# Source scores of every second group gathered from a table in memory instead of looked up with one-hots

## The chip, the core and the metric

The kernel runs on one core of a Trainium2 chip. The metric is the device time of one execution in microseconds. The kernel before takes 1955.77 us, the median of three runs (1955.05 to 1958.15).

## What is computed

Four graph layers follow each other on 1250 nodes with 512 features and 20000 edges, each with a residual sum and a layer norm. The change lies in the second one, graph attention with 8 heads. Its core, cut from the reference:

```
h = (x @ W.T).reshape(n, 8, 64)
e_src = einsum('ehd,hd->eh', h[src], a_src)
e_dst = einsum('ehd,hd->eh', h[dst], a_dst)
e = leaky_relu(e_src + e_dst, 0.2) * (1 + et_emb[edge_type]) * edge_weight
alpha = softmax of e over the edges of a target node
out = scatter_add(dst, h[src] * alpha)
```

For each edge the scores `e_src` (8 numbers that depend on its source node alone) and `e_dst` (8 numbers that depend on its target node) are needed. Each node's scores are small products that the stage before has made.

## The kernel before

The edges are sorted by the block of 128 nodes that holds their target and padded to 176 tiles ("slots") of 128 edges, one edge on a partition. Two slots are a pair with one target block. Stages stand one after another, each a block of programs for the five engines, with a barrier of all engines between two stages.

The stage of the change is `edge_scores` (L1734). It reads the node scores `est` and `edt` (128 partitions x 10 blocks x 8 heads) and fills `es_out` and `ed_out` (128 edges x 176 slots x 8 heads). It goes by groups of four slots, 44 groups in 11 steps of four (`u` = 0 to 3). For one group:

- DVE builds (`build`, L1787, L1792) a one-hot of the source node within its block, a one-hot of the target node within its block, both 128 x 512, and a small one-hot of the source's block.
- PE turns both one-hots (`turn`, L1854, 8 transposes), ACT copies the result to SBUF (L1838).
- PE looks up (`look`, L1865, L1868): the turned source one-hot times the scores of all ten blocks (80 columns, in three bfloat16 parts), the turned target one-hot times those of the pair's block (8 columns, three parts); 24 matmuls in all.
- DVE copies the target scores (L1803), masks the ten candidates of the source with the block one-hot (`mask`, L1805) and sums them (`take`, L1813).

The engines overlap by order: PE turns group g, then looks up g - 1; DVE builds g, masks g - 2, sums g - 3. One-hots, turned one-hots and lookups have two buffers each.

In steps 1 to 8 the stage also mixes the basis of the last layer (`Basis`, L169): 16 pieces of 2 MB are loaded by SP into two buffers (L197), PE multiplies a piece in two halves (L211), one after each lookup, so that a piece takes two groups; ACT copies the results and stores them (L220, L224). SP issues a piece when both halves of the piece before it in the same buffer have been multiplied. GpSimd has no program in the stage. The stage after it, `attention_weights` (L1891), starts with GpSimd's gathers of `h` rows (L674), with an index tile that the changed stage now reads too.

Of the kernel before, what the change touches and what calls it, by code (L numbers as in the profile page):

```python
# [23 lines left out]
P = 128  # L24
N, E, D = 1250, 20000, 512
NB = -(-N // P)
NP = NB * P
# [13 lines left out]
H, DH = 8, 64  # L41
# [1680 lines left out]
GS = 4  # L1722
# [11 lines left out]
def edge_scores(nc, name, C, identb, est, edt, src_lo, src_block, loc, pair_block, es_out, ed_out,  # L1734
                basis):

# [4 lines left out]
    U = 4  # L1741
    STEPS = SLOTS // GS // U
    with ExitStack() as ctx:
# [13 lines left out]
        built, turned, copied, looked = sem("built"), sem("turned"), sem("copied"), sem("looked")  # L1757
        masked, taken = sem("masked"), sem("taken")
        basis.begin(ctx, sem)
        mixing = lambda i: 1 <= i <= Basis.STEPS if isinstance(i, int) else True  # L1760
# [11 lines left out]
        @block.sync  # L1772
        def _(sp):
            basis.load(sp)

        @block.vector
        def _(v):
# [5 lines left out]
            def build(i, u):  # L1783
                wait(v, turned, i * U + (u - 1))
                s = bass.ds((i * U + u) * GS, GS)
                for n, col in ((0, src_lo), (1, loc)):
                    nc.vector.tensor_tensor(oh[:, u % 2, n, :, :],  # L1787
                                            C.f("iota_p").unsqueeze(1).to_broadcast([P, GS, P]),
                                            col[:, s].unsqueeze(2).to_broadcast([P, GS, P]),
                                            ALU.is_equal).then_inc(built, 1)  # L1790
                wait(v, masked, i * U + (u - U + 1))
                nc.vector.tensor_tensor(ohb[:, u, :, :],  # L1792
                                        C.f("iota_p")[:, 0:NB].unsqueeze(1).to_broadcast([P, GS, NB]),
                                        src_block[:, s].unsqueeze(2).to_broadcast([P, GS, NB]),
                                        ALU.is_equal).then_inc(built, 1)

            def mask(i, u):

                g = i * U + u
                v.wait_ge(built, g * 3 + 3)  # L1800
                v.wait_ge(looked, g + 1)
                wait(v, taken, g - 1)
                nc.vector.tensor_copy(ed_out[:, bass.ds(g * GS, GS), :],  # L1803
                                      pl[:, u % 2, ES:ES + ED].rearrange("p (s h) -> p s h", h=H))
                nc.vector.tensor_tensor(  # L1805
                    mine[:, u % 2, :, :, :],
                    pl[:, u % 2, 0:ES].rearrange("p (s b h) -> p s h b", h=H, b=NB),
                    ohb[:, u, :, :].unsqueeze(2).to_broadcast([P, GS, H, NB]), ALU.mult).then_inc(masked, 1)

            def take(i, u):  # L1810
                g = i * U + u
                v.wait_ge(masked, g + 1)
                nc.vector.tensor_reduce(es_out[:, bass.ds(g * GS, GS), :], mine[:, u % 2, :, :, :],  # L1813
                                        AX.X, ALU.add).then_inc(taken, 1)
# [16 lines left out]
        @block.scalar  # L1831
        def _(act):
            def step(i):
                for u in range(U):
                    g = i * U + u
                    act.wait_ge(turned, g + 1)
                    wait(act, looked, g - 1)
                    nc.scalar.copy(ohT[:, u % 2, :, :, :], pT[:, u % 2, :, :, :]).then_inc(copied, 1)  # L1838
                    if mixing(i):
                        basis.store(act, i - 1, u // 2, u % 2)  # L1840
            steps(act, step)
            basis.end_store(act)

        @block.tensor
        def _(pe):
            pe.wait_ge(tables, 1)

            def turn(i, u):
                g = i * U + u
                pe.wait_ge(built, g * 3 + 2)  # L1850
                wait(pe, copied, g - 1)
                for n in range(2):
                    for s in range(GS):
                        ins = nc.tensor.transpose(pT[:, u % 2, n, s, :], oh[:, u % 2, n, s, :], identb[:, :])  # L1854
                ins.then_inc(turned, 1)

            def look(i, u):
# [5 lines left out]
                for s in range(GS):  # L1863
                    for n in range(3):
                        nc.tensor.matmul(pl[:, u % 2, s * NB * H:(s + 1) * NB * H], ohT[:, u % 2, 0, s, :],  # L1865
                                         flat(s3[:, n, :, :]), start=n == 0, stop=n == 2)
# [198 lines left out]
def gnn(nc, ins, consts, out):  # L2065
# [5 lines left out]
    tab = {n: dram(f"tab_{n}", s) for n, s in {  # L2071
        "q": [NP, D], "h": [NP, D],
        "w1": [REL * BCH, D * D // BCH], "w2": [REL * BCH, D * D // BCH]}.items()}
    VECS = ["L0_gnn_b", "L1_gnn_ln_gamma", "L1_gnn_ln_beta", "L2_gnn_bias", "L2_gnn_gamma", "L2_gnn_beta",
            "L3_gnn_bias1", "L3_gnn_bias2"]
    with ExitStack() as top:
# [180 lines left out]
        with ExitStack() as ctx:  # L2257
            es, ed = (ctx.enter_context(nc.sbuf_tensor(f"edge_{n}", [P, SLOTS, H], F32)) for n in ("e_src", "e_dst"))
            edge_scores(nc, "scores", C, identb, est, edt, src_lo, src_block, loc["dst"], pairs["dst"], es, ed, basis[1])
            attention_weights(nc, "att", C, es, ed, factor, loc["dst"][:, :], block_of_pair[:, :],  # L2260
# [88 lines left out]
```

## Time and profile before

| | |
|---|---|
| median of three runs | 1955.77 us |
| profiled execution | 1963.35 us |
| its span | 1961.5 us |
| PE busy | 1613.1 us (82%) |
| DVE busy | 1164.8 us (59%) |
| ACT busy | 471.8 us (24%) |
| POOL (GpSimd) busy | 684.4 us (35%) |

Busy times are sums over the span and come from stages with different limits. The stage of edge scores lies between about 973 and 1114 us. TensorE's granted clock is given as a share of its full speed of 2.4 GHz; 0.5 is the level of 1.2 GHz. PEld is TensorE's weight load, POOL is GpSimd. A name with a q (SPq, POOLq) is the engine's sequencer, which issues transfers and waits.

### The profile page before, as it was taken

What the parts mean: (1) busy time and instruction counts of PE and PEld (TensorE: products, weight loads), DVE (VectorE), ACT (ScalarE), POOL (GpSimd) and SP (SyncE); (2) the same over time, 40 slices, a digit from 0 to 9 for tenths busy, and PEclk for the clock granted to TensorE, in tenths of its full rate; (3) what the DMA queues carried; (4) which work ended last, traced back from release to release, by engine and by line L of the source; (5) the groups of instructions that cost most, each with busy time, mean ns of one, the idle gap of its engine ahead of it and who ended that gap; (6) DMA issues with size and microseconds to landing.
All of it is one profiled execution on the core that took longest, in us unless ns stands there. A gap on an engine that the chain in (4) does not pass through costs nothing. (4 is left out here: it accounts for less than half of the span.)

```text
span 1961.5 us, 27790 instructions
## 1 busy us (share of the span) xinstructions
PE 1613.1 (82%) x7565; PEld 984.4 (50%) x7566; DVE 1164.8 (59%) x2302; ACT 471.8 (24%) x884; POOL 684.4 (35%) x605
## 2 busy tenths in 40 slices
PE   6751886777588999998888639988498899999998
PEld 6641553334443555554555425544245545874486
DVE  5678656886356777776477776665773822113222
ACT  4300112433311555554344310000110111001100
POOL 0002834887265776661000247776340010000000
PEclk9999988999679999999989669999799999999999
DMA  0002885001920776673279327777104301430033
GB/s 25 0 0 86 279 294 189 1 1 54 350 85 38 206 206 187 186 176 71 96 282 353 130 76 210 208 211 188 35 1 129 108 0 38 171 134 1 1 133 134
DMA packets 76201, 248.91 MB, mean 127 GB/s; under 512 B 14758, under 2 KB 28439, under 8 KB 68203
## 3 DMA queue, kind: packets, MB, share of 16 engines
q1 hardware_dynamic: 38474, 147.06, 21.0%
q0 software_dynamic: 34592, 96.87, 18.7%
q10 hardware_dynamic: 3072, 4.20, 0.7%
q8 instruction: 33, 0.54, 0.1%
q14 instruction: 30, 0.24, 0.0%
HBM read 215.91 MB, written 32.00 MB: 126 GB/s over the span
## 5 line engine op out<-in xcount | busy, mean ns | idle before, releaser
L645 POOL DMA_INDIRECT tab_slots<-slot_words,slot_address x160 | 220.5, 1378 | 286.4 <-issue 231.0
L1424 PE MATMUL dense_pY<-weights,dense_xT_block 128*128 128x512 f32 x640 | 284.4, 601 | 0.0
L674 POOL DMA_INDIRECT e_rows<-tab_h,idx_h x176 | 174.9, 994 | 297.8 <-POOLq L50 220.1
L1472 PE MATMUL dense_pY<-parts,dense_number 128*128 128x512 f32 x1000 | 238.4, 400 | 6.9 <-DMA dense_number<-tab_edges_to 6.8
L975 POOL DMA_INDIRECT e_rows<-tab_q,idx_q x192 | 182.4, 950 | 98.5 <-issue 39.8
L1472 PEld LDWEIGHTS dense_pY<-parts,dense_number 128*128 128x128 f32 x1000 | 189.3, 190 | 54.7 <-DMA dense_number<-tab_edges_to 8.0
L768 PE MATMUL e_pS<-e_rows,e_onehot_ring 128*128 128x512 f32 x352 | 195.4, 646 | 21.0 <-DVE e_rows L744 18.5
L1424 PEld LDWEIGHTS dense_pY<-weights,dense_xT_block 128*128 128x128 f32 x640 | 121.6, 194 | 143.5 <-issue 143.2
L1048 PE MATMUL e_pS<-e_rows,e_onehot_f 128*128 128x512 f32 x384 | 181.4, 596 | 0.0
L858 PE MATMUL count_pA<-count_onehot_d,count_onehot_s 128*128 128x512 f16 (+1 forms) x576 | 119.6, 355 | 46.7 <-DVE count_onehot_d L836 44.6
L744 DVE TENSOR_TENSOR e_rows<-e_rows,e_pW 128x1024 f32<-128x1024 f32 x88 | 107.3, 1220 | 68.9 <-DMA e_rows<-tab_h,idx_h 68.9
L992 DVE TENSOR_TENSOR e_rows<-e_rows,e_pP 128x1024 f32<-128x1024 f32 x96 | 117.1, 1220 | 7.4 <-DMA e_rows<-tab_q,idx_q 6.6
L836 DVE TENSOR_SCALAR count_onehot_d<-count_iota,dst_of_src 128x1280 f16<-128x1280 f16 x192 | 109.8, 614 | 18.8 <-PE count_pA L858 17.2
L1442 DVE SCALAR_TENSOR_TENSOR parts<-dense_pY,dense_gates,parts 128x512 fp32r<-128x512 f32 x40 | 28.2, 747 | 146.8 <-ACT parts L1434 146.8
L858 PEld LDWEIGHTS count_pA<-count_onehot_d,count_onehot_s 128*128 128x128 f16 x576 | 56.3, 98 | 110.5 <-issue 97.2
L770 PEld LDWEIGHTS e_pN<-edge_weights,e_onehot_ring 128*128 128x128 f32 x352 | 67.9, 193 | 86.0 <-issue 86.0
L1231 PE MATMUL n_pY<-weights,n_xT_block 128*128 128x512 f32 x240 | 109.6, 608 | 0.0
L1017 ACT ACTIVATE e_rows<-e_rows 128x1024 f32<-128x1024 f32 x96 | 101.7, 1059 | 5.6 <-DVE e_rows L992 5.6
L1001 DVE TENSOR_TENSOR acc<-e_pS,acc 128x512 f32 x96 | 66.4, 692 | 58.2 <-PE e_pS L1048 58.2
L1048 PEld LDWEIGHTS e_pS<-e_rows,e_onehot_f 128*128 128x128 f32 x384 | 72.7, 189 | 55.8 <-issue 47.5
L1651 DVE TENSOR_TENSOR acc<-dense_pY,acc 128x512 f32<-128x512 f32 x20 | 13.8, 692 | 145.9 <-PE dense_pY L1472 145.9
L617 PE MATMUL src_pO<-src_onehot_s,src_onehot_p 125*128 125x192 f32 x320 | 68.1, 366 | 32.7 <-DVE src_onehot_s L606 32.7
(312 smaller groups left out, 2459.8 us busy)
## 6 DMA issues: line engine op xcount, KB each, us to landing
basis_piece<-in_L_gnn_basis_pieces SPq DMA_DIRECT2D x32, 2048.0 KB, 8.0
dense_number<-tab_edges_from SPq DMA_DIRECT2D x20, 1280.0 KB, 5.5
tab_edges_from<-counts_turned SPq DMA_DIRECT2D x10, 1280.0 KB
tab_edges_to<-counts_total SPq DMA_DIRECT2D x10, 640.0 KB
dense_number<-tab_edges_to SPq DMA_DIRECT2D x10, 640.0 KB, 4.6
tab_w<-basis_wout ACTq DMA_DIRECT2D x128, 32.0 KB
weights<-tab_w SPq DMA_DIRECT2D x4, 1024.0 KB, 6.6
weights<-in_L_gnn_W_T SPq DMA_DIRECT2D x3, 1024.0 KB
```

The costliest lines, as they stand in the source:

```text
L645: pool.indirect_dma_start(self.table, bass.IndirectOffsetOnAxis(self.address[:, t:t + 1], 0), self.words[:, t, :], None).then_inc(self.pla ...
L674: pool.indirect_dma_start(self.rows[:, q, s, :], None, self.table, bass.IndirectOffsetOnAxis(self.idx[:, j * 2 + s:j * 2 + s + 1], 0)).the ...
L744: nc.vector.tensor_tensor(r, r, pW[:, bass.ds(i * 16 + u * 2, 2), :].unsqueeze(3).to_broadcast([P, 2, H, DH]), ALU.mult).then_inc(weighted, 1)
L768: nc.tensor.matmul(flat(pS[:, bass.ds(bank[u], 1), :]), ohr[:, u % 4, s, :], rows[:, u, s, :], start=False, stop=True, skip_group_check=True)
L836: nc.vector.tensor_scalar(ohd[:, u % RING, :], iota[:, :], dst[:, bass.ds(t, 1)], None, ALU.is_equal).then_inc(built, 1)
L858: ins = nc.tensor.matmul(flat(pA[:, bass.ds(bank[u], 1), a:b]), ohs[:, h, u, :], ohd[:, u % RING, a:b], start=False, stop=True, skip_group ...
L975: pool.indirect_dma_start(rows[:, q, s, :], None, q_table, bass.IndirectOffsetOnAxis(idx[:, j * 2 + s:j * 2 + s + 1], 0)).then_inc(got[q], 16)
L992: nc.vector.tensor_tensor(rows[:, u, :, :], rows[:, u, :, :], pP[:, u % 2, :, :], ALU.add).then_inc(summand, 1)
L1048: ins = nc.tensor.matmul(pS[:, u % 2, :], ohf[:, u, s, :], rows[:, u, s, :], start=s == 0, stop=s == 1)
L1231: ins = nc.tensor.matmul(py[:, k, w, :], xt[:, k, c, :], weights[w][0][:, c, :], start=c == 0, stop=c == 3)
L1424: ins = self.nc.tensor.matmul(self.banks.at(g), self.xt[:, b % 2, c, :], weights[:, c, :], start=c == 0, stop=c == 3)
L1472: ins = self.nc.tensor.matmul(self.banks.at(self.first + b), self.number[:, b % 2, r * NB + k, :], self.parts[r][n][:, k, :], start=k == 0 ...
```

## The change

The groups with `u` 0 and 2 stay as they are. In the groups with `u` 1 and 3 DVE builds the target one-hot alone, PE turns and looks up only that, ACT copies half as much, and the masking and the sum are left out. For their 88 slots GpSimd gathers the source scores with an indirect DMA for each slot, 128 rows of 8 float32 numbers, from a table in memory. SP writes this table (40 KB) at the start of the stage; GpSimd waits for that, and at the end for all its gathers.

```diff
@@ edge_scores
+        est_out, es_in = sem("est_out"), sem("es_in")
+        looked_up = lambda u: u % 2 == 0
+        built_ahead = (0, 3, 4, 7)
...
         @block.sync
         def _(sp):
+            sp.dma_start(est_table.rearrange("(b p) h -> p b h", p=P), est[:, :, :]).then_inc(est_out, 16)
             basis.load(sp)
+            sp.wait_ge(est_out, 16)
+
+        @block.gpsimd
+        def _(pool):
+            pool.wait_ge(est_out, 16)
+            gathered = [g * GS + s for g in range(STEPS * U) if not looked_up(g % U) for s in range(GS)]
+            for s in gathered:
+                pool.indirect_dma_start(es_out[:, s, :], None, est_table,
+                                        bass.IndirectOffsetOnAxis(idx[:, s:s + 1], 0)).then_inc(es_in, 16)
+            pool.wait_ge(es_in, 16 * len(gathered))
...
             def build(i, u):
...
-                for n, col in ((0, src_lo), (1, loc)):
+                for n, col in ((0, src_lo), (1, loc))[0 if looked_up(u) else 1:]:
...
+                if not looked_up(u):
+                    return
...
             def mask(i, u):
...
+                if not looked_up(u):
+                    ins.then_inc(masked, 1)
+                    return
...
             def take(i, u):
+                if not looked_up(u):
+                    return
...
-                    nc.scalar.copy(ohT[:, u % 2, :, :, :], pT[:, u % 2, :, :, :]).then_inc(copied, 1)
+                    ends = slice(0 if looked_up(u) else 1, 2)
+                    nc.scalar.copy(ohT[:, u % 2, ends, :, :], pT[:, u % 2, ends, :, :]).then_inc(copied, 1)
...
-                for n in range(2):
+                for n in range(0 if looked_up(u) else 1, 2):
                     for s in range(GS):
                         ins = nc.tensor.transpose(pT[:, u % 2, n, s, :], oh[:, u % 2, n, s, :], identb[:, :])
...
-                    for n in range(3):
+                    for n in range(3 if looked_up(u) else 0):
                         nc.tensor.matmul(pl[:, u % 2, s * NB * H:(s + 1) * NB * H], ohT[:, u % 2, 0, s, :],
```

On GpSimd, between the gathers of the first convolution (`e_rows` from `tab_q`) and those of the attention weights (`e_rows` from `tab_h`), the row order now is (the lines moved by up to 22):

```order
 L975 DMA e_rows<-tab_q,idx_q 128x512 x192
 L952 UNCONDITIONAL_BRANCH
-L49 ISA x3
-L1932 UNCONDITIONAL_BRANCH
+L49 ISA x2
+L1781 UNCONDITIONAL_BRANCH
+L1786 DMA edge_e_src<-tab_est,idx_h 128x8 x88
+L1743 UNCONDITIONAL_BRANCH
+L49 ISA
+L1954 UNCONDITIONAL_BRANCH
 L674 DMA e_rows<-tab_h,idx_h 128x512 x16
```

Where GpSimd passed from one barrier to the next, 88 gathers into `edge_e_src` (`es_out`) stand between the two.

On PE, in the loop of the mixing steps, the kernel before has this from one multiply of a piece to the next (`scores_pT` are the transposes, `scores_pLook` the lookups, `basis_ps` the multiplies):

```order
L211 MATMUL basis_ps<-basis_piece,basis_mix 32x512 x4
L1850 ISA
L1854 MATMUL scores_pT<-identb,scores_onehots 128x128 x8
L1859 ISA
L1859 TENSOR_LOAD pair_block_dst
...
L1865 MATMUL scores_pLook<-scores_source,scores_onehotsT 128x80 x3
L1868 MATMUL scores_pLook<-scores_target,scores_onehotsT 128x8 x3
L211 MATMUL basis_ps<-basis_piece,basis_mix 32x512 x4
```

In the changed kernel, from the second multiply of a piece over the first of the next one to its second:

```order
L1876 MATMUL scores_pT<-identb,scores_onehots 128x128 x8
...
L1890 MATMUL scores_pLook<-scores_target,scores_onehotsT 128x8 x4
L207 REGISTER_ALU
L77 REGISTER_ALU
L211 MATMUL basis_ps<-basis_piece,basis_mix 32x512 x4
L1872 REGISTER_ALU
L1876 MATMUL scores_pT<-identb,scores_onehots 128x128 x4
...
L1887 MATMUL scores_pLook<-scores_source,scores_onehotsT 128x80 x3
L1890 MATMUL scores_pLook<-scores_target,scores_onehotsT 128x8 x3
L77 REGISTER_ALU
L211 MATMUL basis_ps<-basis_piece,basis_mix 32x512 x4
```

Between a piece's first and second multiply stand the four transposes of a gathered group and the full lookup of the group before it; between its second and the next piece's first, eight transposes and the short lookup of a gathered group.

## Rows read from the trace of the kernel before

**Rows 1.** Windows: length, busy us (instructions) by engine, clock, DMA share, GB/s.

```profile
970.00:988.60 18.60, 10.22 (x136) 8.90 (x136) 12.70 (x36) 5.11 (x6) 0.00 (x0) 0.57 0.62 241
988.60:1089.00 100.40, 86.97 (x1254) 51.30 (x1251) 71.83 (x189) 47.09 (x62) 0.00 (x0) 0.96 0.83 313
1089.00:1114.00 25.00, 18.08 (x280) 15.81 (x279) 18.61 (x50) 8.58 (x9) 0.00 (x0) 0.63 0.04 7
```

**Rows 2.** Timeline of DVE at the stage's end: start us, us, instruction, idle before.

```profile
1112.25 0.48 DVE L1805 TENSOR_TENSOR scores_of_own_block<-scores_pLook,scores_onehot_block 128x320 f32<-128x320 f32 x1
1112.65 0.87 DVE L1813 TENSOR_REDUCE edge_e_src<-scores_of_own_block 128x32 f32<-128x320 f32 x2
1114.26 0.25 DVE L1961 TENSOR_SCALAR att_mask<-loc_dst 128x176 f32<-128x176 f32 x1 [0.74 <-PEq L50]
```

**Rows 3.** Landing of the basis loads; timeline of their issues, multiplies and transposes.

```profile
DMA to landing us min/median/max: 7.7/8.0/12.5
...
1020.49 6.23 SPq L197 DMA_DIRECT2D basis_piece<-in_L_gnn_basis_pieces  x2
1021.99 1.07 PE L211 MATMUL basis_ps<-basis_piece,basis_mix 128*32 128x512 f32 x8
1022.99 0.62 PE L1854 MATMUL scores_pT<-identb,scores_onehots 128*128 128x128 bf16 x8
1025.10 1.06 PE L211 MATMUL basis_ps<-basis_piece,basis_mix 128*32 128x512 f32 x8
...
1028.58 1.06 PE L211 MATMUL basis_ps<-basis_piece,basis_mix 128*32 128x512 f32 x8 [0.15 <-DMA basis_piece<-in_L_gnn_basis_pieces]
```

**Rows 4.** Timeline of PE: first multiply of the basis, and one group in the tail.

```profile
988.60 1.94 PE L211 MATMUL basis_ps<-basis_piece,basis_mix 128*32 128x512 f32 x8
...
1099.07 1.01 PE L1854 MATMUL scores_pT<-identb,scores_onehots 128*128 128x128 bf16 x8
1100.50 0.36 PE L1865 MATMUL scores_pLook<-scores_source,scores_onehotsT 128*128 128x80 bf16 x3 [0.42 <-DVE scores_of_own_block L1805]
...
1101.77 1.01 PE L1854 MATMUL scores_pT<-identb,scores_onehots 128*128 128x128 bf16 x8
```

**Rows 5.** Lines of GpSimd's indirect DMAs in two stages; shortest scatter by its line.

```profile
L975 POOL DMA_INDIRECT e_rows<-tab_q,idx_q x192 | 182.4, 950 | 98.5 <-issue 39.8 <-PE e_pS L1048 36.4 <-SPq L952 22.3
...
L645 POOL DMA_INDIRECT tab_slots<-slot_words,slot_address x88 | 129.6, 1472 | 75.5 <-POOLq L50 49.0 <-issue 26.5
...
L645 POOL DMA_INDIRECT tab_slots<-slot_words,slot_address x160: 1172/1238/2172, 183.5 to 506.2; - x160
```

**Rows 6.** Timeline of GpSimd and DVE at the start of the next stage.

```profile
1116.14 1.74 POOL L674 DMA_INDIRECT e_rows<-tab_h,idx_h  x1 [0.30 <-issue]
1118.18 1.36 POOL L674 DMA_INDIRECT e_rows<-tab_h,idx_h  x1 [0.30 <-issue]
...
1115.43 1.63 DVE L1966 TENSOR_TENSOR edge_e_src<-edge_e_src,edge_e_dst 128x1408 f32<-128x1408 f32 x1
1117.10 1.62 DVE L1967 SCALAR_TENSOR_TENSOR edge_e_src<-edge_e_src 128x1408 f32<-128x1408 f32 x1
```

**Rows 7.** Timeline of DVE: the builds of one group in the mixing stretch.

```profile
1020.38 0.68 DVE L1787 TENSOR_TENSOR scores_onehots<-const_table,src_lo 128x512 bf16<-128x512 f32 x1
1020.98 0.68 DVE L1787 TENSOR_TENSOR scores_onehots<-const_table,loc_dst 128x512 bf16<-128x512 f32 x1
1021.59 0.19 DVE L1792 TENSOR_TENSOR scores_onehot_block<-const_table,src_block 128x40 f32<-128x40 f32 x1
```

**Rows 8.** Landing of L975; scatter queue, 183 to 300 us; issues: KB, us to landing.

```profile
DMA to landing us min/median/max: 3.3/3.7/7.8
...
q0 software_dynamic: 1792, 0.12, 3.0%
...
basis_mix<-in_L_gnn_att_mix SPq DMA_DIRECT2D x1, 16.0 KB, 1.6
...
tab_slots<-slots_dst SPq DMA_DIRECT2D x1, 176.0 KB, 5.7
```

More of the change, by code:

```diff
@@ L1734, in edge_scores @@
 def edge_scores(nc, name, C, identb, est, edt, src_lo, src_block, loc, pair_block, es_out, ed_out,
-                basis):
+                basis, est_table, idx):
     U = 4
@@ L1799, in mask @@
                 g = i * U + u
-                v.wait_ge(built, g * 3 + 3)
                 v.wait_ge(looked, g + 1)
-                wait(v, taken, g - 1)
-                nc.vector.tensor_copy(ed_out[:, bass.ds(g * GS, GS), :],
-                                      pl[:, u % 2, ES:ES + ED].rearrange("p (s h) -> p s h", h=H))
+                ins = nc.vector.tensor_copy(ed_out[:, bass.ds(g * GS, GS), :],
+                                            pl[:, u % 2, ES:ES + ED].rearrange("p (s h) -> p s h", h=H))
+                if not looked_up(u):
+                    ins.then_inc(masked, 1)
+                    return
+                v.wait_ge(built, i * 8 + (built_ahead[u] + 3))
+                wait(v, taken, i * 2 + (u // 2 - 1))
                 nc.vector.tensor_tensor(
-                    mine[:, u % 2, :, :, :],
+                    mine[:, u // 2, :, :, :],
                     pl[:, u % 2, 0:ES].rearrange("p (s b h) -> p s h b", h=H, b=NB),
@@ L1810, in take @@
             def take(i, u):
+                if not looked_up(u):
+                    return
                 g = i * U + u
                 v.wait_ge(masked, g + 1)
-                nc.vector.tensor_reduce(es_out[:, bass.ds(g * GS, GS), :], mine[:, u % 2, :, :, :],
+                nc.vector.tensor_reduce(es_out[:, bass.ds(g * GS, GS), :], mine[:, u // 2, :, :, :],
                                         AX.X, ALU.add).then_inc(taken, 1)
@@ L1849, in turn @@
                 g = i * U + u
-                pe.wait_ge(built, g * 3 + 2)
+                pe.wait_ge(built, i * 8 + (built_ahead[u] + (2 if looked_up(u) else 1)))
                 wait(pe, copied, g - 1)
-                for n in range(2):
+                for n in range(0 if looked_up(u) else 1, 2):
                     for s in range(GS):
@@ L2071, in gnn @@
     tab = {n: dram(f"tab_{n}", s) for n, s in {
-        "q": [NP, D], "h": [NP, D],
+        "q": [NP, D], "h": [NP, D], "est": [NP, H],
         "w1": [REL * BCH, D * D // BCH], "w2": [REL * BCH, D * D // BCH]}.items()}
@@ L2258, in gnn @@
             es, ed = (ctx.enter_context(nc.sbuf_tensor(f"edge_{n}", [P, SLOTS, H], F32)) for n in ("e_src", "e_dst"))
-            edge_scores(nc, "scores", C, identb, est, edt, src_lo, src_block, loc["dst"], pairs["dst"], es, ed, basis[1])
+            edge_scores(nc, "scores", C, identb, est, edt, src_lo, src_block, loc["dst"], pairs["dst"], es, ed, basis[1],
+                        tab["est"], idx["h"])
             attention_weights(nc, "att", C, es, ed, factor, loc["dst"][:, :], block_of_pair[:, :],
```

## The prediction

> **What bounds the kernel now.** The page's chain of waits only reaches back to 1383 us, so the place of the change is read from other views. First the windows: all edited lines belong to one stage, the edge scores, which an all-engine barrier closes on both sides. It fills 973.1 to 1114.3 us, and GpSimd is busy for 0.00 us in it [rows 1]. What the stage gains or loses at its end passes in full to what follows, since DVE's first instruction of the next stage waits on the barrier [rows 2].
>
> Three stretches have different limits. In the lead-in (970 to 988.6) and the tail (1089 to 1114) TensorE's granted clock averages 0.57 and 0.63, and PE works through one group after another: in the tail its transposes start at 1099.07 and the next group's at 1101.77, 2.70 us for a group, of which 2.28 are matmuls [rows 4]. DVE and ACT have gaps there and wait for PE.
>
> Between them lies the mixing stretch, 100.4 us long, in which the basis of the last layer passes in 16 pieces of 2 MB beside the groups, two groups to a piece. PE is busy for 86.97 us of it [rows 1], but it is not what sets the pace. Piece 6 is issued at 1020.49, when the last multiply of piece 4 is over, and its first multiply starts at 1028.58, released by its DMA: 8.1 us, where the loads' median landing is 8.0. Piece 7's issue lies between the end of piece 5's second multiply (1025.10 + 1.06 = 1026.16) and 1020.49 + 6.23 = 1026.72, say at 1026.4 [rows 3]. Two buffers make a loop: two periods are one landing (8.1) plus the time from a piece's first multiply to the issue that its second one releases (1021.99 to 1026.4, 4.4). That is 12.5 us for two, 6.2 us a piece; 16 of them are the 100 us. Only what shortens those 4.4 us, or the landing, helps there.
>
> **The change part by part.** Of 44 groups of four tiles, 22 lose one of two one-hots, 4 of 8 transposes, 12 of 24 lookup matmuls, half of ACT's copy, the block one-hot, the masking and the reduce. GpSimd gets 88 indirect gathers of 128 rows of 32 bytes, SP one store of 40 KB ahead of the basis loads.
>
> *PE, lead-in.* At this clock a gathered group saves half of 1.01 us of transposes and half of the 1.27 us from 1100.50 to 1101.77, that is 0.50 + 0.64 = 1.14 us [rows 4]. Two of the four groups are gathered; the transposes of group 1 lie beside ACT's copy of group 0, so 2 x 1.14 - 0.50 = 1.8 us go. The pieces needed next are there in time: the first load is followed by its landing of 8 us from 973.5, and it was first used at 988.6. SP's store ahead of it costs a fraction of a microsecond of a slack of some 5; were the slack gone, it would cost that much once.
>
> *PE, mixing.* Inside the 4.4 us stand the gathered group's transposes (0.62 us at this clock, half goes [rows 3]) and the lookup of the other group, which stays. The gathered group's own lookup stands outside. So 0.31 us a loop, 0.16 a period, 2.2 us over 14 periods. Against it the gathers pass through the DMA engines with the loads. The nearest rows are the 56 scatters beside the first basis: 3.0% of 117 us, 3.5 us in all, 0.063 us each [rows 8]. A landing of 8.1 us would see some 6 gathers, 0.37 us, again half of it per period: 0.18. I take zero for the stretch, with -2.2 (no interference) and +2.8 (twice the scatters' price) as ends. The DVE and ACT work saved here is worth nothing: DVE is busy for 71.83 and ACT for 47.09 of the 100.4 us [rows 1], and what they do lies beside the landings.
>
> *PE, tail.* Eight groups, four gathered: 4 x 1.14 = 4.6 us. The last group is a gathered one, so one multiply (0.48 us) and one reduce go from the end, together about 0.8 us after overlap [rows 2]. That is 5.4 us.
>
> Sum on this path: -1.8 + 0 - 5.4 = -7.2 us; DVE's last instruction moves from 1113.5 to about 1106.3.
>
> *GpSimd.* The new wait: nothing but the gathers is queued behind it on GpSimd, and the closing barrier waits for all 88 landings. The store is issued at 973.1; the nearest rows for its landing are 1.6 us (the basis mix, a 16 KB load) and 5.7 us (the slot table) [rows 8]. I take 3.4, so GpSimd starts at about 977. A gather of 2 KB rows takes 0.95 us and the next one starts 0.30 later [rows 5, 6]; a scatter of 8 bytes takes 1.17 us at the least and 1.47 on average in the counting stage [rows 5]. The operation here is a gather of 128 rows, as the one at 0.95, so I take that for the bare instruction: 1.25 us from start to start.
>
> To this comes DVE. The gather at 1116.14 took 1.74 us and ended 0.82 after the DVE instruction with two SBUF inputs that began before it (1115.43 + 1.63 = 1117.06), although the next DVE instruction was running by then; the one at 1118.18 ended 0.82 after that next one [rows 6]. So a gather that starts under such an instruction waits for its end, once. The 192 gathers of the first convolution, where DVE's second input is in PSUM, average 0.95 [rows 5]. The builds of the one-hots here are of the harmful kind, both inputs in SBUF: for each pair of groups 3 x 0.68 + 0.19 = 2.2 us remain of 6.2 [rows 7], 36%, with half of 0.68 left on average: 0.12 us a gather. 1.37 x 88 = 121 us; 977 + 121 + 3.7 of landing [rows 8] = 1101.7. That is 4.6 us before the other path's end, so the gathers are hidden, with little to spare.
>
> Bounds: bare gathers give 977 + 110 + 3.7 = 1091, hidden by far. With the scatter's price of the counting stage, 1.47 + 0.30 = 1.77, GpSimd ends at 977 + 156 + 3.7 = 1136.5, 23 us later than the stage now ends. The break-even with 1113.5 is (1113.5 - 3.7 - 977) / 88 = 1.51 us a gather.
>
> The Trainium skill, page "SBUF — State Buffer", section "Who interferes with whom", says that a VectorE instruction with two SBUF inputs contends with a GpSimd instruction that reads SBUF, and that the second to issue is blocked until the first is done. The two delayed gathers agree with it; the result of its own that it could give is the second rival.
>
> **Time.** The profiled execution took 1963.35 us, 1.85 more than its span, and 7.6 above the median 1955.77. The stage's differences are small and carry over as they are: 1955.8 - 7.2 = 1948.6 us.
>
> **Rivals.**
> 1. *GpSimd becomes the stage's end* (slower). Place: the closing barrier waits for the last gather. If an indirect DMA of small rows costs what the shortest scatter does, 1.17 us, the step is 1.17 + 0.30 + 0.12 = 1.59; 977 + 140 + 3.7 = 1120.7, +7 us, 1963; by the scatters' average of 1.47 it is the +23 above. It decides from 1.51 us on. For it: the only indirect DMAs with short rows in the trace are the dearer ones. Against: those write to memory, from 125 partitions, and the gathers of 128 rows take 0.95.
> 2. *No change*. Two builds and the block one-hot follow each other with starts 0.60 us apart, each before the last has ended [rows 7]. If GpSimd isn't let in between them, they act as one block of 1.4 us: (1.4² + 0.68²) / 2 / 6.2 = 0.20 us a gather, and in the tail, where a pair takes some 4.2 us, 0.29. With the landing behind 16 KB basis packets at twice its usual 3.7, GpSimd ends at 977 + 88 x 1.46 + 7.4 = 1113. For it: the starts overlap. Against: the gather after 1117.06 got in within a gap of 0.04. The same time comes out if the loads' landing grows by 1 us through the gathers: 14 x 0.5 = 7.
> 3. *The clock falls in the mixing stretch* (slower). PE has less to do there: some 4.7 us of 6.2. In the tail, where the basis multiplies are gone, the granted clock dropped to 0.63 on average. With all at the lower level a piece takes 2 x 1.94 (multiplies) + 1.01 + 0.50 + 1.27 + 0.64 and some 0.8 of gaps = 8.1 us [rows 4], 16 x 1.9 = +30 us, 1978 with the gains. Against: the multiplies, which set the level at the stretch's beginning, all stay.
> 4. *More gain*: interference is nil and the first of the tail's gaps, where PE waits for ACT's copy, close too: -7.2 - 2.2 - 3 = -12, 1943.
>
> That the change doesn't do what it says is excluded for counts by the order: 88 gathers stand on GpSimd.
>
> **How the numbers follow.** Forecast 45%, rival 1 17%, rival 2 22%, rival 3 7%, rival 4 9%. A measurement tells 0.2%, 3.9 us, from nothing; the forecast and rival 4 are faster by more, 0.54; rival 2 is 0.22; rivals 1 and 3 are 0.24. The forecast's own range, by the mixing stretch's ends, is 1946 to 1952. The range over the cases leaves out most of rival 3 and the far end of rival 1: 1941 to 1966.
>
> **What would show it.** In the changed profile: first basis multiply near 986.8; pieces still issued 6.0 to 6.4 us apart; the last multiply of the basis near 1087; gathers starting near 977 and 1.3 to 1.45 us apart, some lengthened by up to 0.7 us under builds; the last one landed before DVE's last reduce, which ends near 1106. Wrong: a gather row with a median above 1.2 us, GpSimd as the last to reach the barrier, a piece period off by over 0.3 us, or a granted clock below 0.9 in the mixing stretch.

## The result, and the profile after

The changed kernel is slower: 1965.83 us, the median of nine runs (1961.53 to 1974.39), against 1955.89 (1953.84 to 1960.11) for the kernel before on the same chip. The medians are 9.9 us apart. The ratio used below, which is not their quotient, is 1.0055 with an interval of 1.0038 to 1.0072, about 10.8 us. The forecast was 1948.6, faster by 7.2; the time lies at the upper end of the range, and on the other side.

The profiled execution of the changed kernel took 1961.53 us (span 1959.6), the shortest of the nine, so its trace shows less of the loss than the median does. The stage begins some 5 us earlier in it than in the trace of before (what precedes it differs from run to run), so lengths are compared, not positions. First the windows, cut at the first and last multiply of the basis; columns as in [rows 1].

```profile
968.00:982.20 14.20, 8.35 (x104) 6.97 (x104) 9.91 (x28) 4.11 (x5) 8.98 (x9) 0.50 0.82 303
982.20:1090.80 108.60, 86.50 (x1009) 44.40 (x1006) 51.68 (x128) 39.94 (x62) 79.56 (x79) 0.83 0.86 292
1090.80:1114.00 23.20, 14.10 (x208) 11.57 (x204) 12.20 (x33) 6.88 (x9) 0.00 (x0) 0.63 0.04 8
```

Lead-in and tail are shorter than in [rows 1], though by less than forecast. The mixing stretch grew from 100.4 to 108.6 us. PE is as busy in it as before, 86.5 against 87.0 us, with 1009 matmul records in place of 1254: a fifth of the work went, and the rest took longer at a granted clock of 0.83 in place of 0.96. Over the whole stage, from DVE's first instruction in it to the next stage's first, it is 145.6 us (967.95 to 1113.55) against 141.1 (973.14 to 1114.26). Two of the signs that the prediction named came: the clock is below 0.9, and pieces are issued 6.82 us apart on average (14 issues from 987.9 to 1076.5) in place of 6.37.

The gathers themselves went as forecast. Here is their line (ns min/median/max, first and last start), then the timelines of GpSimd, its last gather and its first instruction of the next stage, and of DVE at the end of the stage.

```profile
L1786 POOL DMA_INDIRECT edge_e_src<-tab_est,idx_h x88: 940/944/1462, 970.5 to 1084.7; - x88
```

```profile
1084.65 0.94 POOL L1786 DMA_INDIRECT edge_e_src<-tab_est,idx_h  x1 [0.30 <-issue]
1114.19 0.94 POOL L674 DMA_INDIRECT e_rows<-tab_h,idx_h  x1 [28.59 <-POOLq L50]
...
1112.30 0.47 DVE L1834 TENSOR_REDUCE edge_e_src<-scores_of_own_block 128x32 f32<-128x320 f32 x1
1113.55 0.25 DVE L1983 TENSOR_SCALAR att_mask<-loc_dst 128x176 f32<-128x176 f32 x1 [0.77 <-PEq L50]
```

The median gather takes 0.944 us, as the one in [rows 5], some up to 1.46 us; 88 in 115 us make 1.31 us each, where 1.37 was forecast. 17 of them took over 1 us, and each of these ended 0.81 to 0.82 us after the end of a DVE build that was running when it began:

```profile
1064.76 0.68 DVE L1801 TENSOR_TENSOR scores_onehots<-const_table,loc_dst 128x512 bf16<-128x512 f32 x1
1064.80 1.46 POOL L1786 DMA_INDIRECT edge_e_src<-tab_est,idx_h  x1 [0.30 <-issue]
```

GpSimd then waits 28.6 us. It is nowhere near the end of the stage.

What became of the basis loop of [rows 3] is in the timeline of the changed kernel around pieces 10 and 11:

```profile
1046.96 1.94 PE L211 MATMUL basis_ps<-basis_piece,basis_mix 128*32 128x512 f32 x8
1049.11 6.67 SPq L197 DMA_DIRECT2D basis_piece<-in_L_gnn_basis_pieces  x2
1050.45 1.06 PE L211 MATMUL basis_ps<-basis_piece,basis_mix 128*32 128x512 f32 x8 [0.63 <-DMA basis_piece<-in_L_gnn_basis_pieces]
1052.07 1.01 ACT L1860 COPY scores_onehotsT<-scores_pT 128x1024 bf16<-128x1024 bf16 x1 [2.52 <-PE scores_pT L1876]
1053.13 0.28 PE L1887 MATMUL scores_pLook<-scores_source,scores_onehotsT 128*128 128x80 bf16 x3 [1.28 <-ACT scores_onehotsT L1860]
1054.17 1.07 PE L211 MATMUL basis_ps<-basis_piece,basis_mix 128*32 128x512 f32 x8
```

The multiply in the first row takes 1.94 us, the length of [rows 4] at the lower level, in the middle of the stretch. And after a DMA wait PE waits 1.28 us more for ACT's copy. The windows, cut where the granted clock changes, show the first of these:

```profile
1035.40:1045.60 10.20, 7.19 (x96) 3.82 (x95) 5.18 (x13) 4.32 (x7) 7.76 (x9) 1.00 0.87 308
1045.60:1049.00 3.40, 3.39 (x34) 1.69 (x35) 1.31 (x4) 0.87 (x3) 2.79 (x3) 0.51 0.97 401
1049.00:1059.30 10.30, 7.19 (x98) 3.82 (x97) 5.18 (x13) 4.44 (x7) 7.86 (x9) 1.00 0.90 304
1059.30:1062.70 3.40, 3.40 (x35) 1.69 (x36) 1.37 (x4) 0.76 (x3) 2.49 (x4) 0.50 1.00 402
```

PE was busy for 7.19 of 10.2 us at the full clock, then the clock was granted at half, PE was busy without a pause, and the clock came back. After the clock first rose, seven such falls lie in the mixing of the changed kernel's trace (from 994.5, 1008.1, 1032.0, 1045.7, 1059.3, 1073.0 and 1086.6) and one in that of before (from 1003.1).

The waits for landings grew too. Of the line of the basis multiplies in the two kernels, the idle time that a load ended (us, times), first before, then after:

```profile
  DMA basis_piece<-in_L_gnn_basis_pieces: 2.6, 5
```

```profile
  DMA basis_piece<-in_L_gnn_basis_pieces: 5.5, 10
```

But in this one trace the landings themselves hardly grew: from the issue of pieces 4 to 15 to their first multiply it took 8.44 us on average, against 8.24 before (issues and multiplies of the two timelines). What it shows of the loss is mostly the clock.

### The profile page after: what moved, and what is told of

The parts are those of the page before. It is cut to its first block and busy times, and to the rows that moved or that the text cites. A ratio compares the mean times of both kernels' runs of the same rounds, so it can differ in the third digit from the quotient of the medians.

```text
span 1959.6 us, 26997 instructions
## 1 busy us (share of the span) xinstructions
PE 1604.0 (82%) x7213; PEld 970.5 (50%) x7214; DVE 1135.0 (58%) x2214; ACT 462.0 (24%) x884; POOL 773.8 (39%) x693
## 5 line engine op out<-in xcount | busy, mean ns | idle before, releaser
L975 POOL DMA_INDIRECT e_rows<-tab_q,idx_q x192 | 182.2, 949 | 98.8 <-issue 39.5
L1786 POOL DMA_INDIRECT edge_e_src<-tab_est,idx_h x88 | 88.5, 1006 | 107.4 <-DMA tab_est<-e_src 80.8
L211 PE MATMUL basis_ps<-basis_piece,basis_mix 128*32 128x512 f32 x512 | 79.8, 699 | 26.2 <-DMA basis_piece<-in_L_gnn_basis_pieces 26.0
```

The source lines that it names most:

```text
L975: pool.indirect_dma_start(rows[:, q, s, :], None, q_table, bass.IndirectOffsetOnAxis(idx[:, j * 2 + s:j * 2 + s + 1], 0)).then_inc(got[q], 16)
```

## The experiments

Two theories stood. Theory A: with less to do PE is granted the lower clock in the mixing stretch. Theory B: the gathers lengthen the landing of the basis loads, which the loop waits for. Kernels of one group ran on one chip, each ratio is to the kernel before on that chip, in five rounds. Medians of before there: 1955.47 us for the first four kernels, 1957.07 for the second four, 1957.11 for the last four. "Mixing" (first to last multiply of the basis) and clock are from the one profiled execution of each; there the kernel before has 100.4 us and 0.96, the changed kernel 108.6 and 0.83.

| kernel | median us | ratio (interval) | mixing us | clock |
|---|---|---|---|---|
| e1 no gathers | 1957.58 | 1.0012 (1.0001 to 1.0024) | 106.4 | 0.85 |
| e2 before + 88 gathers | 1964.75 | 1.0051 (1.0033 to 1.0069) | 107.9 | 0.95 |
| e3 PE's work kept | 1962.13 | 1.0029 (1.0018 to 1.0040) | 108.7 | 0.94 |
| e4 steps 0, 9, 10 gathered | 1961.06 | 1.0028 (1.0018 to 1.0039) | 109.6 | 0.95 |
| e5 no gathers, PE's work kept | 1952.81 | 0.9989 (0.9974 to 1.0003) | 98.3 | 0.99 |
| e6 before + 88 gathers, rows apart | 1966.41 | 1.0042 (1.0028 to 1.0057) | 107.7 | 0.95 |
| e7 24 gathers, 16 after the loads | 1958.98 | 0.9999 (0.9986 to 1.0012) | 100.0 | 0.97 |
| e8 before + 88 plain loads | 1961.45 | 1.0016 (1.0004 to 1.0029) | 103.1 | 0.94 |
| e9 before, half loads | 1956.11 | 0.9997 (0.9987 to 1.0007) | 100.1 | 0.96 |
| e10 after, half loads | 1957.20 | 0.9999 (0.9989 to 1.0009) | 104.8 | 0.84 |
| e11 e7, half loads | 1953.35 | 0.9983 (0.9974 to 0.9992) | 101.0 | 0.97 |
| e12 e3, half loads | 1952.75 | 0.9984 (0.9974 to 0.9993) | 98.6 | 1.00 |

**e1: the changed kernel without its gathers.**

```diff
-            for s in gathered:
-                pool.indirect_dma_start(es_out[:, s, :], None, est_table,
...
+            nc.gpsimd.memset(es_out[:, :, :].rearrange("p (g a s) h -> p g a (s h)", a=2, s=GS)[:, :, 1, :], 0.0)
```

> The changed kernel with GpSimd's 88 gathers left out (their slots are set to zero by one GpSimd memset instead, so those source scores are missing); SP's store of the table stays. Theory A (PE, with less to do in the mixing stretch, is granted the lower clock in repeated short stretches, which lengthens the pieces' period): the gathers have no part in it, the time stays near the changed kernel's, +6 to +10 us against the kernel before, and the granted clock of the mixing stretch stays near 0.85. Rival B (the gathers' traffic lengthens the landing of the basis loads): the loss goes away and the savings at both ends remain, -3 to -7 us.

Neither forecast was met: most of the loss goes with the gathers, from 1.0055 to 1.0012, yet no gain comes out. The window of its mixing stretch:

```profile
981.70:1088.10 106.40, 85.11 (x1009) 43.52 (x1007) 51.41 (x128) 39.90 (x63) 0.00 (x0) 0.85 0.79 295
```

Without a single gather the stretch is 6 us longer than before, at a clock of 0.85. So B alone doesn't explain the trace. PE's waits for loads are 3.6 us in it, with landings of 8.0 in the median: part of the 5.5 above comes without any gather.

**e2: the kernel before with the gathers beside it.**

```diff
+            for n, s in enumerate(gathered):
+                pool.indirect_dma_start(aside[:, n, :], None, est_table, ...)
```

> The kernel before with the store of the table and the same 88 gathers added, into a tile that nothing reads; all lookups stay. Theory A: PE's work is that of before, the clock of the mixing stretch stays near 0.96 and the time within 0 to +2.5 us of the kernel before (what the gathers cost the loads). Rival B: +6 to +10 us.

All of PE's work is there, the clock is 0.95, and the kernel is still 0.5% slower, as rival B has it: A alone doesn't explain it either. The table's store, which this kernel has too, isn't the reason: from the stage's start to the first multiply it takes 15.44 us, before 15.46. PE's waits for loads in the stretch:

```profile
  DMA basis_piece<-in_L_gnn_basis_pieces: 8.0, 9
```

That is 8.0 us against 2.6 before. From the issue of pieces 4 to 15 to their first multiply it took 9.24 us on average, up to 11.3, where it took 8.24 in the trace of before. Piece 11 is the longest:

```profile
1047.04 7.22 SPq L197 DMA_DIRECT2D basis_piece<-in_L_gnn_basis_pieces  x2
...
1058.33 1.89 PE L211 MATMUL basis_ps<-basis_piece,basis_mix 128*32 128x512 f32 x8 [2.51 <-DMA basis_piece<-in_L_gnn_basis_pieces]
```

How a load is held up can be looked for in the DMA queues, here from 1.0 to 3.0 us after the issue of piece 11 (1047.04): share of the 16 engines.

```profile
q0 software_dynamic: 48, 0.01, 24.1%
q1 hardware_dynamic: 7, 0.05, 14.5%
q10 hardware_dynamic: 50, 0.06, 8.7%
```

The load's queue (q1) holds 84.7% of the engines between 1020 and 1028 us of the kernel before. Here it got 14.5%, the gathers 24.1, and half of the engines' time shows no packet at all. So in this stretch the load waits without the engines being full; why, the trace doesn't show.

**e3: the changed kernel with PE's old number of transposes and lookups** (the extra ones read the target one-hots, their results are not used).

```diff
-                for n in range(0 if looked_up(u) else 1, 2):
+                for n in range(2):
...
-                    for n in range(3 if looked_up(u) else 0):
+                    for n in range(3):
```

> The changed kernel with PE's transposes and lookup matmuls kept at their old number in the gathered groups (the extra ones turn and look up the target one-hot into places that nothing reads); DVE, ACT and GpSimd work as in the changed kernel. Theory A: the clock returns to about 0.96 in the mixing stretch, and with PE's chain as long as before the time is -1 to +2 us against the kernel before. Rival B: the loss of the mixing stretch stays and the savings of the ends go too: +8 to +12 us.

More work for PE makes the kernel faster, from 1.0055 to 1.0029, at a clock of 0.94. The rest of the loss stays, with the gathers; the time lies between the two forecasts. The mixing lengths of the two traces don't show the gain, 108.7 against 108.6: from issue to first multiply it took 9.33 us on average in this trace and 8.44 in that of the changed kernel, its shortest execution.

**e4: all groups of steps 0, 9 and 10 gathered, none of the mixing steps.**

```diff
-        looked_up = lambda u: u % 2 == 0
+        looked_up = lambda i: not isinstance(i, int) or 1 <= i <= last_mixed
...
```

> All 12 groups of steps 0, 9 and 10, outside the mixing stretch, are gathered (48 gathers); the 32 groups beside the basis keep their lookups. Theory A: the mixing stretch stays at about 100 us and clock 0.96; the lead-in gains 2 to 3 us, the tail 0.7 us a group, 5 us: -6 to -8 us. Rival B: 48 gathers over the first 60 us of the mixing stretch cost about half of the changed kernel's 8 us there, so -2 to -4 us.

Both forecasts were gains, and it is a loss: 48 gathers, issued one after another from the stage's start on (967.9 to 1030.9), cost 0.3%. The trace has the clearest hold-up of all. Piece 8 is issued at 1023.86, and its first multiply starts at 1037.73, 13.9 us later (timeline; the multiply at 1027.35 is that of piece 7):

```profile
1023.86 20.13 SPq L197 DMA_DIRECT2D basis_piece<-in_L_gnn_basis_pieces  x3
1027.35 1.06 PE L211 MATMUL basis_ps<-basis_piece,basis_mix 128*32 128x512 f32 x8 [1.91 <-DMA basis_piece<-in_L_gnn_basis_pieces]
...
1037.73 1.94 PE L211 MATMUL basis_ps<-basis_piece,basis_mix 128*32 128x512 f32 x8 [2.91 <-DMA basis_piece<-in_L_gnn_basis_pieces]
```

The DMA view of 1026 to 1029 in this kernel, and below it that of 1044 to 1047, when the gathers are over:

```profile
DMA packets 92, 0.04 MB, mean 14 GB/s; under 512 B 76, under 2 KB 76, under 8 KB 92
...
q0 software_dynamic: 61, 0.01, 88.3%
q10 hardware_dynamic: 28, 0.03, 3.0%
q1 hardware_dynamic: 3, 0.00, 0.1%
...
DMA packets 147, 1.19 MB, mean 398 GB/s; under 512 B 40, under 2 KB 40, under 8 KB 79
...
q1 hardware_dynamic: 84, 1.11, 97.0%
```

For three microseconds 61 packets of gathers occupy 88% of the engines, and the load stands still: its queue's three packets (q1) hold 0.00 MB. The gathers' packets are long in time, not in bytes. The Trainium skill, page "DMA: Bandwidth & Descriptors", section "Queues, rings and completion order", says that each DMA engine takes packets from its queues in turn. By that rule a load beside slow packets would still get every second one; in these rows it got none of its data, and the measurement decides.

**e5: no gathers and PE's work kept**, the edits of e1 and e3 together.

> The changed kernel without its 88 gathers (GpSimd sets those slots to zero instead, so their source scores are missing) and with PE's transposes and lookups at the old number; what DVE and ACT save stays. Theory A (with less work PE is granted the lower clock in the mixing stretch, which is why leaving out the gathers alone gave 1957.6 and no gain): with PE's work back the low stretches go, the mixing stretch returns from 106.4 to about 100.5 us, and the time is 1953 to 1956, at least 2 us below the kernel without gathers. Rival C (it is the new order of waits, the lookup behind ACT's copy, not the clock): the mixing stretch stays near 106 us at a high clock and the time near 1957.6.

```profile
983.70:1082.00 98.30, 84.97 (x1253) 50.23 (x1251) 51.45 (x128) 39.87 (x62) 0.00 (x0) 0.99 0.85 319
```

Against e1 only work on PE was added, and the mixing stretch is 8.1 us shorter: the clock is granted at 0.99. Theory A holds as one of two causes; rival C falls.

**e6: e2 with rows that lie 2 KB apart**, from the table of the first convolution.

```diff
-                pool.indirect_dma_start(aside[:, n, :], None, est_table, ...idx...)
+                pool.indirect_dma_start(aside[:, n, :], None, wide, ...far...)
```

> The kernel before plus 88 gathers of 32-byte rows into a tile that nothing reads, as in the experiment that gave 1964.8, but the rows are the first 32 bytes of 2 KB rows of a 2.6 MB table (that of the first convolution) and not neighbours in 40 KB; one small DVE instruction makes the indices, the 40 KB store stays and its table is unread. Theory B1 (the DMA engines stop because one gather's 128 rows all hit the same small piece of memory): no stretch without basis packets in mid-load, landings back to about 8.2 us, 1956 to 1958. Theory B2 (any small rows from the software queue do it): as before, some landings of 9 to 11 us, 1963 to 1967.

1.0042, an interval that overlaps with that of e2, and 9.32 us on average from issue to first multiply: it isn't the small table. B1 falls.

**e7: 24 gathers, 8 in the lead-in, 16 after the last piece has landed.**

```diff
+        looked_up = lambda i, u: not isinstance(i, int) or 1 <= i <= Basis.STEPS or u % 2 == 0
...
+                if s == gathered[2 * GS]:
+                    for k in range(2):
+                        pool.wait_ge(basis.loaded[k], Basis.STEPS * 16)
...
```

> The changed kernel with only 24 gathers, all results right: groups 1 and 3 of the lead-in (8 gathers, at the stage's start) and groups 1 and 3 of the last two steps (16 gathers, which GpSimd issues after the last two basis pieces have landed); all 32 groups of the mixing steps keep their lookups. If gathers harm only beside basis loads and PE's full work keeps the clock in the mixing stretch: lead-in -1.2 and tail -2.6 us as in the changed kernel's profile, mixing 100 to 101 us, in all 1951 to 1953, a ratio near 0.998; GpSimd's last landing some 2 us before the barrier. Rival: the eight gathers of the lead-in delay the first pieces, or the 16 late ones reach the barrier last: 1955 to 1959.

Not slower any more, but not faster: the rival's time. In its trace the stage is as expected: mixing 100.0 us at a clock of 0.97, and from the stage's first DVE instruction to the next stage's 137.2 us (971.36 to 1108.52) against 141.1 before. The median shows none of that; its twelve runs lie between 1951.63 and 1961.28. Whether the profiled execution was a good one or something later gives the gain back was not settled.

**e8: e2 with plain loads** of the same size in place of gathers.

```diff
-                pool.indirect_dma_start(aside[:, n, :], None, est_table, ...)
+                pool.dma_start(aside[:, n, :], est_table[n % NB * P:(n % NB + 1) * P, :])
```

> The kernel before plus the 40 KB store and 88 plain loads by GpSimd, each 128 neighbouring rows of 32 bytes of the small table, into a tile that nothing reads. Theory B3 (the indirection on GpSimd's queue is what stops the basis packets): landings at about 8.2 us, 1955 to 1957. Theory B2 (small rows do it, however they are asked for): landings of 9 to 11 us as with the gathers, 1963 to 1967. GpSimd's pace for a plain load isn't in any trace so far; if it is under 1 us the same number of loads lies beside fewer pieces.

Between the two: 1.0016. GpSimd issues them in 0.66 us each, from 972.5 to 1018.5, so they lie beside seven pieces, not fourteen, and half of e2's loss would be 1.0025. The ratio doesn't tell indirection from small rows, but the trace speaks for small rows: pieces 3 to 6, issued from 997.2 to 1018.0, took 9.56, 9.94, 9.77 and 10.39 us to their first multiply (8.1 to 9.1 in the trace of before), and the nine pieces after them 7.96 to 8.43. This is piece 5:

```profile
1011.82 6.54 SPq L197 DMA_DIRECT2D basis_piece<-in_L_gnn_basis_pieces  x2
...
1021.59 1.93 PE L211 MATMUL basis_ps<-basis_piece,basis_mix 128*32 128x512 f32 x8 [1.87 <-DMA basis_piece<-in_L_gnn_basis_pieces]
```

So B3 as it stands, landings of about 8.2 us without the indirection, isn't borne out. The longest packet of these loads took 0.70 us, against 1.45 of a gather in e2.

**e9 to e12: the basis in halves.** A half of a piece is loaded again as soon as its own multiply is over; the same edit in the kernel before, the changed kernel, e7 and e3.

```diff
+                    for s in range(2):
+                        wait(eng, self.used, i * 4 + (k * 2 + s - 3))
+                        f = slice(s * BW // 2, (s + 1) * BW // 2)
+                        eng.dma_start(self.piece[:, k, f], self.pieces[..., f]
+                                      ).then_inc(self.loaded[k * 2 + s], 16)
...
```

> The kernel before with one change, in this stage alone: a basis piece is loaded in two halves of 1 MB, and a half is loaded again as soon as its own multiply is over, where a whole piece waited for both. If the loop of landing and multiplies is what set the stretch's pace: four multiplies now lie between a half's multiplies, so the landing is hidden; PE (87 us of work) and the transfers (128 packets of 0.61 us on 16 engines, 4.9 us a piece, plus 0.35 of stores) remain: 5.6 to 5.9 us a piece in place of 6.2, mixing 90 to 94 us, in all -6 to -10 us, ratio 0.995 to 0.997. Rival: PE or the transfers already set it, or smaller rows cost the loads as much: no change, 1955 to 1958.

> The changed kernel, all 88 gathers, with the basis loaded in halves. If its loss is that the gathers lengthen landings which the loop waits for: hidden now, the mixing stretch is near that of the kernel before with half loads and the lead-in and tail keep their 3.8 us, so it is 3 to 5 us faster than that one, 1943 to 1948, ratio 0.992 to 0.995. Rival A (PE with less to do gets the lower clock in any case, more so when it is the bound): low stretches stay, mixing 98 to 104 us, the time within 3 us of the kernel before or above.

> Only 24 gathers, in the lead-in and after the last piece has landed, and the basis in halves. PE keeps all its work in the mixing steps, so the clock stays up: the mixing stretch as in the kernel before with half loads, and the stage's ends 4 us shorter as in this kernel's trace with whole loads: 1944 to 1949. Rival: as with whole loads the shorter ends don't show in the time, then equal to the kernel before with half loads; or the stage now ends so early that the late gathers (21 us and 3.7 of landing after the last piece) reach the barrier last, up to 3 us over it.

> The changed kernel with PE's transposes and lookups at the old number and the basis in halves: all gathers, but no loss of clock for want of work. If both mechanisms are as read, it lies at the kernel before with half loads, within 3 us (what DVE and ACT save against what the gathers still cost), 1946 to 1952. If the gathers slow the transfers themselves by more than the loop's slack hides (they held the engines for up to 4.5 us at a time), it stays 4 us or more above that one.

In all four traces no multiply waits for a load. The times of e9 to e11 lie above what was forecast for the theory, that of e12 0.75 us above. e9 gains nothing: PE's own chain is as long as the loop was. In its timeline PE waits for ACT's copy after the multiply and the transposes:

```profile
1030.95 1.01 ACT L1847 COPY scores_onehotsT<-scores_pT 128x1024 bf16<-128x1024 bf16 x1 [2.02 <-PE scores_pLook L1877]
...
1032.20 0.27 PE L1874 MATMUL scores_pLook<-scores_source,scores_onehotsT 128*128 128x80 bf16 x3 [0.62 <-ACT scores_onehotsT L1847]
```

But the same edit takes the changed kernel from 1.0055 to 0.9999 and e3 from 1.0029 to 0.9984: the gathers' harm is the landing on the path, and it goes when the landing is hidden. What is left of e10 is the clock. The mixing windows of e10 and of e12, which differ in PE's work alone:

```profile
981.10:1085.90 104.80, 85.08 (x1010) 43.75 (x1007) 51.81 (x128) 39.83 (x62) 79.50 (x79) 0.84 0.92 302
```

```profile
981.60:1080.20 98.60, 84.49 (x1252) 50.38 (x1251) 51.53 (x128) 39.93 (x62) 76.23 (x74) 1.00 0.92 322
```

PE is as busy with 1010 matmuls as with 1252. e11 and e12 are faster than the kernel before by 0.17 and 0.16%, some 3 us, with intervals below 1. That is little: their intervals overlap with that of e9, the kernel before with the same loads. In e11 DVE's last instruction ends at 1105.84 and the next stage starts 1.3 us later, 0.5 more than in the changed kernel: which fits the late gathers coming in last, by about that.

## Why the prediction was wrong

The step that failed is "I take zero for the stretch": it charged a gather for its share of the DMA engines alone, and the sum had no term for the clock. The stretch grew by 8.2 us in the profiled execution, and by more than that if the ratio is gone by, which is 10.8 us up although the stage's ends gained some 3.8. Two mechanisms did it that stood among the rivals, the landing as a second form of rival 2 (22%), the clock as rival 3 (7%), each taken alone. In the one trace of the changed kernel it is mostly the clock; that the landing belongs to its loss rests on the ratios with and without gathers and on the traces of e2, e3 and e6.

*The landing.* The step priced a gather by its share of the DMA engines, 0.063 us from [rows 8], and let 0.37 us fall on a landing. As a share that was no bad guess: in the 96 us from 989 on, the gathers' packets took 6.4% of the engines' time, 6.1 us for the 74 issued there, 0.083 each. But the share isn't the price: beside gathers a load is now and then held up for microseconds, in e4 with the engines full of the gathers' packets, in e2 with half of the engines' time empty. Leaving the gathers out takes 0.43% from the changed kernel (e1) and 0.40% from e3 (e5), 8 us; adding them to the kernel before costs 0.51%, 10 us. By the intervals each of these is known to some 0.2%, 4 us. The second rival had this as its other form, "loads' landing grows by 1 us through the gathers: 14 x 0.5 = 7", and 9.24 against 8.24 us in e2 is that microsecond. Its consequence fell short: it was to cancel a gain of 7.2 us, but the ends gave 3.8 and the clock took more than that.

*The clock.* The third rival was given 7% with "the multiplies, which set the level at the stretch's beginning, all stay". They stay in the changed kernel, too, and the level fell all the same. Nor do they alone set it: in e12 the clock rose at 980.10, before the first multiply (981.58), after PE had been busy for 4.94 of 5.10 us with transposes and lookups. It fell in part, to a mean of 0.83, not to the lower level throughout, so it cost 4.5 us (e1 against e5, 0.23%) to 5.1 (the changed kernel against e3, 0.26%) in place of 30, each net of what PE's shorter ends give and each known to some 0.2%, 4 us; e10 against e12 gives 0.15%, and in the traces e1 and e5 differ by 8.1 us of mixing. The trace of before gave a hint in [rows 1]: PE at 87% busy with a clock of 0.96, not 1.00.

*Together.* e5 has neither and stands at -0.11%, -2.2 us. -2.2 + 4.5 + 7.8 = 10.1 us; the changed kernel measured 10.8. Within the intervals, 4 us, the two add up, and a third cause isn't needed.

*What bounds the stretch.* "Only what shortens those 4.4 us, or the landing, helps" was half right. A second bound lay just under the loop, PE's chain of multiply, transposes, ACT's copy and lookup (e9: 100.1 us without landings). For the same reason "worth nothing" was perhaps off for the work that DVE and ACT save: with PE's work unchanged the stretch takes 98.3 and 98.6 us (e5, e12). But these are also the traces with the clock at 0.99 and 1.00, so the two are not told apart.

*Lead-in and tail.* -1.8 was forecast for the lead-in; from the stage's first DVE instruction to the first multiply it is 14.26 us (967.95 to 982.21) against 15.46 (973.14 to 988.60), -1.2. (The 0.57 of [rows 1] takes in 3 us ahead of the stage; in the stage, from 973.00 to 988.60, the lead-in ran at 0.50.) -5.4 was forecast for the tail; from the last multiply of the basis to the next stage's DVE it is 22.7 against 25.3 us, -2.6. The timeline of PE in the changed kernel's tail shows a full group and a gathered one in 4.79 us, where 2 x 2.70 [rows 4] minus 1.14 is 4.26 (the pair took 5.31 before, 1099.07 to 1104.38):

```profile
1094.56 0.28 PE L1887 MATMUL scores_pLook<-scores_source,scores_onehotsT 128*128 128x80 bf16 x3 [2.32 <-ACT scores_onehotsT L1860]
...
1100.62 1.01 PE L1876 MATMUL scores_pT<-identb,scores_onehots 128*128 128x128 bf16 x8
1101.83 0.89 PE L1890 MATMUL scores_pLook<-scores_target,scores_onehotsT 128*128 x12 [0.20 <-DVE scores_of_own_block L1824]
1102.58 0.58 PE L1876 MATMUL scores_pT<-identb,scores_onehots 128*128 128x128 bf16 x4
1104.14 0.36 PE L1887 MATMUL scores_pLook<-scores_source,scores_onehotsT 128*128 128x80 bf16 x3 [0.97 <-ACT scores_onehotsT L1860]
...
1105.41 1.01 PE L1876 MATMUL scores_pT<-identb,scores_onehots 128*128 128x128 bf16 x8
```

Half the lookup matmuls take 0.89 us, not half of 1.27, and the shorter transposes open a wait of 0.97 for ACT's copy of the full group. The tail's first pair saved nothing, 4.78 us (1090.76 to 1095.54) against 4.80 (1088.91 to 1093.71): PE waits 2.32 us there for ACT's copy (first row), and the clock, which the prediction took at the lower level for all groups, was full up to 1095.3 in the trace of before. The lead-in has such waits for ACT, too, of 0.68 and 0.83 us.

*GpSimd.* Right in pace and interference, and in the start but for a microsecond: 2.6 us after the store's issue (967.91 to 970.51), where 3.9 was taken. The first rival fell, with 28.6 us to spare before the next stage, less the last gather's landing. So did the second one's first form, builds that act as one block: a gather that began under the first of two builds ended 0.81 to 0.82 us after that one's end (1050.89 to 1052.01, the builds ending at 1051.19 and 1051.79).

## What to carry to other kernels

Before moving work to gathers (or to any loads of small rows), see whether a load that someone waits for passes beside them: price them by what a landing grew, not by their bytes or their share of the engines, and hide that landing first (reloading each half of a buffer as soon as it was used was enough here). Taking work from PE in a stretch that it doesn't bound can cost clock; look for low stretches in the granted clock before calling such a saving free. And two rivals that don't exclude each other need a case in which both happen.

## What the runs showed of the hardware

- Gathers of 32-byte rows can hold a load out of the DMA engines: 61 packets with 88.3% of 16 engines' time for 3 us, at 14 GB/s (e4). The longest single gather packet in e4's trace took 1.96 us, the median one 0.018. The Trainium skill, page "DMA: Bandwidth & Descriptors", section "Latency and other measured facts", gives 2 us for an access to memory at high load, against 0.2 on average. The longest packet is near the first figure; whether it is the same thing no run here shows. Why packets are slow in bursts stays open, as does why a load waits where the engines are half empty (e2): it isn't the small table (e6), and plain loads of such rows lengthen landings, too, without such long packets (e8).
- A gather that GpSimd starts under a DVE instruction with two inputs in SBUF ends 0.81 to 0.82 us after that instruction (so did each of the 17 of the changed kernel's 88 gathers that took over 1 us), even when the next build is already running.
- With 1009 matmuls in place of 1254 in the mixing stretch PE is busy for the same 86 us: the clock took back what was saved.
- A 1 MB half of a piece lands 5.5 us after its issue (median in e9), a 2 MB piece after 8.0.
